# Edge counting in a graph layer: one-hots built by 16-bit comparisons of several steps, digits scaled by ScalarE, and a new order of the steps

## The reference

```
h = x @ W                                   # 1250 x 768
e = leaky_relu(e_src[src] + e_dst[dst])     # one value for each of 41250 edges (+ one self loop per node)
w = exp(e - max over the edges of one dst)
out[dst] = sum over its edges of h[src] * w / z[dst]
x = x + gat(relu(gat(layernorm(x), ...)))
```

## Time and profile before

| | |
|---|---|
| three runs | 1528.14, 1528.83, 1533.79 us |
| profiled execution | 1530.04 us, of which the span from first to last instruction is 1528.3 us |
| busy over the span | PE 92%, PE weight loads 87%, VectorE 76%, ScalarE 63%, GpSimd 32% |
| granted TensorE clock, mean | 0.972 |

### The profile page before, as it was taken

The page is one execution under the profiler, slowest core; times in us unless marked ns, Lnnn a source line. Parts: engine busy times, 40 slices in busy tenths (PEclk is TensorE's granted clock), DMA queues, the critical chain, the costliest instruction groups (busy, mean ns, idle before and its releaser), DMA issues.

```text
span 1528.3 us, 25668 instructions
## 1 busy us (share of the span) xinstructions
PE 1411.6 (92%) x8981; PEld 1336.4 (87%) x8981; DVE 1153.9 (76%) x1756; ACT 969.3 (63%) x1658; POOL 492.4 (32%) x366
## 2 busy tenths in 40 slices
PE   3998799999799999999999999999999998699996
PEld 1897577999699999899898998999988898599996
DVE  5788979735689762486877878778788787788885
ACT  7997787523368432366848767478587522599995
POOL 1000000000000010244625536256356501288886
PEclk9999799999899999999999999999999998799999
DMA  7001000122214540000000000000001496466652
GB/s 201 2 1 37 5 14 18 52 99 73 101 55 131 182 142 22 1 21 1 1 21 0 21 0 0 21 0 0 21 1 32 119 295 169 126 155 163 164 94 35
DMA packets 52312, 99.09 MB, mean 65 GB/s; under 512 B 10848, under 2 KB 26852, under 8 KB 52224
## 3 DMA queue, kind: packets, MB, share of 16 engines
q1 hardware_dynamic: 39769, 72.55, 15.4%
q0 software_dynamic: 11376, 22.29, 7.4%
q10 hardware_dynamic: 1079, 3.13, 0.7%
HBM read 67.15 MB, written 44.31 MB: 73 GB/s over the span
## 4 chain that ended last, share of the span: by engine, by line
PE 68%; DVE 9%; issue 3%; DMA 1%; ACT 1%; POOL 1%; POOLq 0%; SPq 0%; ACTq 0%; DVEq 0%
PE ps L372 14%; PE ps L373 14%; PE ps L374 14%; PE ps L823 4%; PE ps L864 4%; PE ps L843 3%; PE ps L866 3%; PE ps L845 3%; PE ps L865 3%; DVE mcol L1072 2%; PE ps L1257 1%; PE ps L598 1%; DVE prlo L1035 1%; PE ps L832 1%; PE ps L1669 1%
## 5 line engine op out<-in xcount | busy, mean ns | idle before, releaser
L1035 POOL TENSOR_TENSOR prlo<-prob,prhi 125x500 fp32r<-125x500 f32 x180 | 251.7, 1404 | 267.4 <-ACT prob L976 266.2
L1072 DVE TENSOR_REDUCE mcol<-ps 125x1 f32<-125x1250 f32 x120 | 174.9, 1458 | 72.6 <-PE ps L823 72.0
L974 ACT ACTIVATE prhi<-ps 125x500 fp32r<-125x500 f32 x300 | 176.9, 590 | 71.0 <-PE ps L845 64.9
L864 PE MATMUL ps<-prhi,vhi 125*128 125x250 f32 x600 | 172.2, 287 | 8.5 <-POOL prlo L1035 4.3
L976 ACT ACTIVATE prob<-ps 125x500 f32<-125x500 f32 x300 | 176.5, 588 | 0.6 <-DVE prlo L1035 0.6
L1524 POOL MEMSET q<- 128x2500 f32 x1 | 2.2, 2187 | 529.4 <-PE ps L374 529.4
L866 PE MATMUL ps<-prlo,vhi 125*128 125x250 f32 x600 | 168.6, 281 | 0.0
L865 PE MATMUL ps<-prhi,vlo 125*64 125x250 f32 x600 | 167.6, 279 | 0.0
L843 PE MATMUL ps<-qst,kst 128*125 128x250 f32 x600 | 155.9, 283 | 3.5 <-issue 1.4
L372 PE MATMUL ps<-hhi,pthi 125*125 125x384 f32 x400 | 153.6, 384 | 3.0 <-DVE ptlo L712 3.0
L1669 PE MATMUL ps<-ohs,ohd 128*125 128x417 bf16 x380 | 126.1, 384 | 32.4 <-DVE ohs L2112 29.6
(11 more groups left out here) (330 smaller groups left out, 4023.1 us busy)
## 6 DMA issues: line engine op xcount, KB each, us to landing
w1all<-in_L_ffn_W_dram SPq DMA_DIRECT2D x8, 1152.0 KB, 10.1
w2st<-in_L_ffn_W_dram SPq DMA_DIRECT2D x8, 1152.0 KB, 6.6
wqst<-in_L_ffn_Wqkv_dram SPq DMA_DIRECT2D x12, 384.0 KB, 4.2
hid_d<-tin SPq DMA_DIRECT2D x10, 375.0 KB
hin<-hid_d SPq DMA_DIRECT2D x10, 375.0 KB
vtin<-xn_d SPq DMA_DIRECT2D x10, 375.0 KB
out_dram<-accr POOLq DMA_DIRECT2D x10, 375.0 KB, 8.8
xres<-in_x_dram SPq DMA_DIRECT2D x10, 336.0 KB
```

Of the source, the lines that this page charges most:

```text
L864: pe.matmul(ps[:, b:b + GQ], vhi[:, e, kt, :], hi, start=kt == 0, stop=False)
L974: act.activation(prhi[:, n % RING, :], bank(3 + n % 3, P, 2 * GQ), ACT.Exp, scale=float(HD) ** -0.5)
L1035: eng.tensor_tensor(prlo[:, n % RING, :], prob[:, n % 3, :], prhi[:, n % RING, :].bitcast(f32), ALU.subtract)\
L1072: dve.tensor_reduce(mcol[:, e, t:t + 1], ps[0:P, 0:N], AX.X, ALU.max, negate=True).then_inc(sem("max"), 1)
```

## The change

The one-hots of both sides are now plain comparisons of two 16-bit tensors on VectorE, several steps in one instruction. `iota2` holds each column number twice, `drel` and `scol` are f16 in place of f32, and the two steps of a pair lie interleaved, element by element. `destinations(b)` writes 14, 12 or 12 steps at once (30 instructions of 1750 or 1500 elements, ring of 4); the sources are written 4 steps at once (10 instructions per tile, the last with 2 steps; ring of 3). The digit `sval` no longer goes into `ohs`: ScalarE multiplies it into `ohd`, in place, one instruction for each step (`valued`, in place of `apart`), and PE waits for `valued` at each step. PE reads both one-hots with a step of two elements. Edges are the first DMAs, x tile 0 and W follow on the same queue, and the chain that makes `scol` and `sval` is ahead of the test of the edges. Row tiles now take 8 steps each from g = 8 (was 13 from 31), the first turn begins at g = 111 (was 208) and a turn takes 36 steps (was 32), with other slots for its parts.

```diff
-WIDE = 420
-BATCH = WINDOW // 2
-OHS = 12
+DST_AT, DST_WIDE, DSTS = (0, 14, 26, WINDOW), 14, 4
+SRC_WIDE, SRCS = 4, 3
-FIRST, PERIOD = 31, 13
-TURN0, TURN, EARLY, SLOTS = 208, 32, 12, 21
-AHEAD = 30
+FIRST, PERIOD, PARTS = 8, 8, 13
+TURN0, TURN, EARLY, SLOTS = FIRST + 103, 36, 12, 21
+AHEAD = 20
+COUNT_READY = 8
 def linear(t, r):
-    return FIRST + PERIOD * t + r
+    return FIRST + PERIOD * (PARTS * t + r) // PARTS
+WEIGHT1_AT = (2, 3, 5, 6, 9, 10)
...
-    ohs = put("ohs", [128, OHS, WIDE], bf16, at=WEND)
-    scol = put("scol", [128, NCOLS], f32, at=put.end)
-    drel = put("drel", [128, T, WINDOW], f32, at=put.end)
+    ohs = put("ohs", [128, SRCS, SRC_WIDE // 2, PACK, 2], bf16, at=WEND)
+    ohd = put("ohd", [128, DSTS, DST_WIDE // 2, P, 2], bf16, at=ohs_end)
+    iota2 = put("iota2", [128, PACK, 2], f16, at=put.end)
+    scol = put("scol", [128, NCOLS], f16, at=put.end)
+    drel = put("drel", [128, T, WINDOW], f16, at=put.end)
...
 PE, step_near:
-                pe.wait_ge(sem("oh_ready"), g + 1)
-                pe.matmul(into, hots(b)[:, i, :], ohs[:, g % OHS, 0:PACK], start=u == 0, stop=u == WINDOW - 1).then_inc(sem("oh_free"), 1)
+                if i == 0:
+                    pe.wait_ge(sem("oh_ready"), b + 1)
+                pe.wait_ge(sem("valued"), g + 1)
+                pe.matmul(into, hot_dst(g), hot_src(g), start=u == 0, stop=u == WINDOW - 1).then_inc(sem("oh_free"), 1)
...
 ScalarE:
-                last = act.activation(hots(b)[:, i, :], iota[:, 0:P], ACT.Identity, bias=drel[:, j, u:u + 1])
+                act.activation(hot_dst(g), hot_dst(g), ACT.Copy, scale=sval[:, q:q + 1]).then_inc(sem("valued"), 1)
...
 VectorE, destinations and step_near:
-                dve.tensor_scalar(hots(b), hots(b), 0.0, None, ALU.is_equal).then_inc(sem("ohd_ready"), 1)
+                dve.tensor_tensor(ohd[:, b % DSTS, 0:pairs, :, :],
+                                  iota2[:, 0:P, :].rearrange("p (o c) z -> p o c z", o=1).broadcast_to([128, pairs, P, 2]),
+                                  drel[:, j, DST_AT[i]:DST_AT[i + 1]].rearrange("p (b o z) -> p b o z", o=1, z=2)
+                                  .broadcast_to([128, pairs, P, 2]), ALU.is_equal).then_inc(sem("ohd_ready"), 1)
-                if g >= OHS:
-                    dve.wait_ge(sem("oh_free"), g + 1 - OHS)
-                dve.tensor_scalar(ohs[:, g % OHS, :], iota[:, 0:WIDE], scol[:, q:q + 1], sval[:, q:q + 1], ALU.is_equal, ALU.mult)\
+                if b >= SRCS:
+                    dve.wait_ge(sem("oh_free"), src_end(b - SRCS))
+                dve.tensor_tensor(ohs[:, b % SRCS, 0:wide // 2, :, :], iota2[...], scol[:, q:q + wide] ..., ALU.is_equal)
...
 VectorE, first_layer:
-                        if g == (linear(t - 2, 1) if t >= 2 else 6 + 14 * t):
+                        if t and g == linear(t - 2, 1):
                             rstd1(t)
-                        if g == turn_at(t - 2, 2):
-                            leaky(dve, 0, t)
-                        if g == turn_at(t - 3, 5):
+                        if g == turn_at(t - 2, 16):
                             far_max(dve, order, 0, t)
+                        if g == turn_at(t - 2, 20):
+                            leaky(dve, 0, t)
-                        if g == turn_at(t - 2, 17):
+                        if g == turn_at(t - 1, 4):
                             weigh(dve, 0, t)
 PE: turned(t) from turn_at(t - 1, 0) to turn_at(t - 1, 6);  ScalarE: sloped(t) from turn_at(t - 2, 1) to turn_at(t - 2, 16)
```

More of the change, by code:

```diff
@@ L79, in count_bank, with dst_batch, dst_start, src_batch @@
     return 2 if j % 2 == 0 and counted_at(j) + 12 < turn_at(-1, 0) else 3
+def dst_batch(g):
+    j, u = divmod(g, WINDOW)
+    i = sum(u >= at for at in DST_AT[1:-1])
+    return 3 * j + i, u - DST_AT[i]
+def dst_start(b):
+    return WINDOW * (b // 3) + DST_AT[b % 3]
+def src_batch(g):
+    j, u = divmod(g, WINDOW)
+    return SRC_BATCHES * j + u // SRC_WIDE, u % SRC_WIDE
+def src_end(b):
+    return WINDOW * (b // SRC_BATCHES) + min(SRC_WIDE * (b % SRC_BATCHES + 1), WINDOW)
 class Order:
@@ L206, in build @@
     lohi = put("lohi", [128, 3, ECOLS], f32, at=put.end)
+    digit = put("digit", [128, 3, NCOLS], f32, at=put.end)
     xres = put("xres", [P, 2, D], f32, at=W2AT)
@@ L337, in two, with hot_dst, hot_src @@
             return ps[0:rows, b * BANK:(b + 2) * BANK].rearrange("p (a c) -> p a c", a=2)[:, :, 0:cols]
-        def hots(b):
-            return ohd2[:, :, :] if b % 3 == 2 else ohd[:, b % 3, :, :]
+        def hot_dst(g):
+            b, i = dst_batch(g)
+            return ohd[:, b % DSTS, i // 2, :, i % 2]
+        def hot_src(g):
+            b, i = src_batch(g)
+            return ohs[:, b % SRCS, i // 2, :, i % 2]
         def rows(j):
@@ L1352, in _ @@
             weights2(1)
-            for t in range(5):
+            for t in range(7):
                 row_out(t)
[L1355 to L1358, removed]
+            for k in range(2, KD):
+                weights2(k)
+            row_out(7)
             row_in(0)
             row_in(1)
-            row_out(7)
             row_out(8)
@@ L1699, in first_layer @@
                     for j in range(T):
-                        if not near and g == counted_at(j) + 18:
+                        if not near and g == counted_at(j) + COUNT_READY:
                             tile_all(j)
                     for t in range(T):
-                        if g == (linear(t - 1, 0) if t else FIRST - 7):
+                        if t and g == linear(t - 1, 0):
                             transposes1(t)
-                        if 0 <= g - linear(t, 0) < 2 * KD:
-                            triple1(t, g - linear(t, 0))
+                        for i in range(2 * KD):
+                            if g == linear(t, i):
+                                triple1(t, i)
                     if g == NINE + 2:
@@ L1809, in _ @@
             stats(0)
-            stats(1)
-            act.wait_ge(sem("set_pool"), TABLES)
-            for g in range(BATCH):
-                apart(g)
-            for g in range(BATCH, AHEAD):
-                apart(g)
+            act.wait_ge(sem("start_dve"), VALUES)
+            for g in range(4):
+                valued(g)
+            normed(0)
+            for g in range(4, 8):
+                valued(g)
+            higher1(0)
+            for k in range(KD):
+                weights1(k)
+                if k % 2:
+                    valued(7 + k // 2 + 1)
+            for g in range(11, 16):
+                valued(g)
+            stats(1)
+            for g in range(16, AHEAD):
+                valued(g)
             for g in range(SCHEDULE):
@@ L2151, in first_layer @@
                         dve.sem_inc(sem("oh_free"), WINDOW)
-                    if g in range(4, 4 * KD + 4, 4):
-                        weight1(g // 4 - 1)
+                    for b in range(2, 3 * T):
+                        if g == max(dst_start(b) - 26, 0):
+                            if near:
+                                destinations(b)
+                            else:
+                                dve.sem_inc(sem("ohd_ready"), 1)
+                    if g in WEIGHT1_AT:
+                        weight1(WEIGHT1_AT.index(g))
                     for t in range(T):
-                        if g == (linear(t - 2, 1) if t >= 2 else 6 + 14 * t):
+                        if t and g == linear(t - 2, 1):
                             rstd1(t)
-                        if g == (linear(t - 1, 12) if t else FIRST - 2):
+                        if g == (linear(t - 1, 12) if t else 1):
                             lower1(t)
```

167 lines of the change are left out of this document (86 added, 81 removed).

## The result

The changed kernel takes **1563.07 us** (median of 4 runs, 1561.38 to 1565.96) beside 1528.84 us before, a ratio of 1.0223 with a 95% interval of 1.0209 to 1.0237: slower by 34 us, where I had forecast 1513. The profiled execution took 1561.38 us with a span of 1559.1. All ratios in this document leave out slow executions, and so does the median of the run with `stats(1)` early, of whose six executions one took 2792.54 us (with it the median is 1535.16).

A forecast was written before the change was run, and what follows sets the result against it. Bounds: VectorE and ScalarE nearly always busy at the start, PE in row tiles, VectorE in turns with steps. Start -6.1, row tiles -8.0, hole -15.4, turns +13.9 give -15.6 us: 1514.4, or 1513 against the median; range 1506 to 1520, wider 1500 to 1529.

The forecast's parts named there:

- the price of the one-hots: VectorE's one-hot work per tile of 38 steps: 12.15 us with the new comparisons, 12.8 us before.
- I take 0.545: VectorE's new 16-bit comparison: 0.545 ns per element, taken from `ohs`, between ends of 0.26 and 1.03.
- The comparison runs at the f32 rate: Rival, 10 in 100: VectorE's one-hots at 1.03 ns per element, 22.1 us a tile, 1595 us in all, slower.
- my 19.0: Turns with 36 steps: 19.0 us each, VectorE the bound at 18.65, PE 18.0, ScalarE 17.6.
- 7.44 equal turns: Turns after the hole: 268/36 = 7.44 at 19.0 us, then 2.56 at 11.63; 170.6 us, 13.9 more than before.
- Turns keep their losses: Rival, 17 in 100: turns still lose 2.3 us over VectorE's work, 20.95 us each; 14.5 us of gain gone, 1527.5.
- The idle 11 us in `rstd1(1)`: Start: VectorE idle from 18.8 to 29.8 us, as `rstd1(1)` waits for `stats(1)` on ScalarE.
- the first triple: End of the start: first triple can start at 37.8 us instead of 43.9, 6.1 us less.
- The row tiles: Ten row tiles after the start: PE bound at 8.4 us each, 87.7 us in all, 8.0 less than before.
- ScalarE's parts up to the end of `stats(1)`: Start, from 19.4 us: `higher1(0)`, six parts of W, eight `valued`, then `stats(1)`, ending at 29.8 us.
- the hole: From the last row tile's end to turn 0: 22.9 us instead of 38.3, 15.4 less; first turn at 148.4 us.
- the wait for the sources of step 112: End of the hole: step 112 waits for the 834-element batch behind `far_max(1)`, a batch and `leaky(1)`, 4.9 us.

The follow-up runs named there:

- the run with turns of 38 and 18 steps: Against the kernel before: changed kernel plus even first columns, `stats(1)` directly behind `stats(0)`, turns of 38 steps, `COUNT_READY` 18 instead of 8; 1526.26 us (0.9983).
- the next run: Changed kernel with first columns rounded down to even and `stats(1)` on ScalarE directly behind `stats(0)`; 1534.00 us, 1.0038 of the kernel before.

## Why the prediction was wrong

**The step that failed** is the one in the price of the one-hots: "I take 0.545". For tiles 0 to 2 and 7 to 9 it was right (0.52). For tiles 3 to 6 the rate was 1.04, which is the rate of my rival *The comparison runs at the f32 rate*, in four tiles of ten. I had treated the rate as one property of the instruction, with one chance. It is a property of each operand's address too, and the addresses stood in the code: `STARTS` has four odd entries, and a pair of `scol` read from there does not begin on 4 bytes. The comparisons at this rate add 36 x 0.87 = 31.3 us of VectorE, all behind 150 us, and 1.8 us more in the four short ones. Nearly all of this lies in four turns of which VectorE is busy 98.0 of 98.7 us. Putting them right gave back 23.6 us (26.3 between the traces). The trace of before holds no such instruction; what could have been done is to ask for each operand in which tiles it may fall to the other end, and to put a case between 1513 and 1595 into the range.

The page that I set against my value (the Trainium skill, Vector Engine (DVE) Microarchitecture Reference, 5.1) says also that 4-byte alignment makes no difference with two sources; the comparisons with `iota2` or `ohd` shifted agree (1.02 and 1.07 us), those with the pairs of `scol` shifted do not (1.89), and the measurement decides. The Trainium skill (VectorE: DVE Perf Modes, Mode 2×_1P) asks for 4-byte alignment; by that the odd tiles are slow, as measured, and the shifted `iota2` should have been too, which it was not.

**The turns, beyond the rate.** With even columns five turns from 158 to 253 us took 18.5 to 19.6 us each, so my 19.0 stands as a number. My reason for it, that VectorE is the bound, does not: from 177.4 to 253.5 us VectorE was busy 18.2 us a turn and PE 18.7, for which I had 18.0, and the turn from 215.43 us took 18.47 us with PE busy all of it. In the run with turns of 38 and 18 steps PE waits for `ohs` nowhere from 150 to 290 us, while VectorE waits for PE:

```profile
DVE ohs L2164 <- PE ps L1710: 8.3, 8, 1.9
```

That 19.0 came out is in part luck. What I also had wrong is that all turns are alike: I counted 7.44 equal turns and then 11.63. The one from 253.5 to 274.5 us took 21.0, the next 23.0, the next, nearly without steps, 15.7. Turns of 38 steps took 8 us off (7.6 with odd columns). This is the first rival, *Turns keep their losses*, by another mechanism, and its 14.5 us were more than the 8 that came.

**The start.** The idle 11 us in `rstd1(1)` were predicted and are there. The cast and `iota2` were not: I had no term for GpSimd's new instruction. `drel` was 3.2 us later than I had it, and the first triple 3.8. The row tiles (85.5 for 87.7 us) gave 2.2 us of that back. Two of my sums don't add up as stated: 2.5 and 2 us beyond ten tiles of 8.4 give 88.5 us for the row tiles, not 87.7, and ScalarE's parts up to the end of `stats(1)` give 29.4 us, not 29.8.

**Right as sized:** `valued`, 428 ns long and 0.29 apart (13 in 3.91 us); the PE bound row tiles; the hole, with PE's clock at 0.71 in it; the wait for the sources of step 112 ahead of turn 0. With even columns the turn 0 that follows the hole took 8.3 us for its first 10 steps, not 5.3 (19.0 x 10 / 36): its granted clock was 0.50 (1.2 GHz) from 149.8 to 157.0 us and 1.00 behind, after the hole in which PE was busy 12.9 of 22.7 us. I had no term for that. Nor had I one for PE's strided operands: the count matmul takes 350 ns at the median where it took 341, 9 ns in each of 380, or 3.4 us of PE in all.

**The sum.** 50.1 us of miss: 23.6 from the odd columns (26.3 by the traces); 7.6 to 8.4 from the turns of 36; 1.4 from the start as it reaches turn 0; about 3 from the cold beginning of turn 0. Behind the first layer the profiled run lost 1.6 us more than before, and its median lies 1.7 us above it, where before it was 1.2 below. That leaves some 6 to 10 us, in part the wait for `hin` (2.2 us), that I can't settle. What also stays open: in the run with even columns the median is 3.3 us above the profiled run. A fall of the clock in the turn from 274.5 us, as in the trace of the next run (2.6 us), may be a part of it; no trace of this kernel shows it.

## What to carry to other kernels

When a price rests on a faster rate, list for each operand the tiles in which its address or shape could take it out of that rate; a window that begins at a rounded column is even only by luck. Look at the shortest and longest of a group before its mean: 1369 ns was no duration of any instruction here. If two loops are woven together, a period that does not match the other's (36 and 38) is harmless at first and costs at the end, and a new small instruction on an idle engine has to be priced too.

## What the runs showed of the hardware

A 16-bit comparison of two tensors on VectorE, 1668 elements in and out, takes 1.02 us, and 1.89 when the source that repeats a pair begins 2 bytes past a multiple of 4; the same shift of the other source changes nothing, nor does that of the output in the comparisons of 1500 and 1750 elements. GpSimd's iota of 834 elements with each number twice took 4.65 us, while 1252 numbers each once took 1.18 to 1.33. The copy on VectorE that replaced the first took 1.00 us, with small GpSimd instructions beside it. PE's granted clock fell to 0.50 for 3 to 7 us behind a wait of 3.22 us in two traces, and not behind the same wait in a third. VectorE's cast of 768 numbers, 0.56 us alone, ended only 0.41 or 0.42 us after the iota that it met, in three kernels. The Trainium skill (SBUF — State Buffer, 🔬 SBUF: two separate sides) has the port pair that the two engines share as an exclusive lock for the whole instruction of whichever starts first, where VectorE's instruction is in a two-port mode. These traces agree, if the cast is such a one: the iota began first in all three, by 0.3 to 3.2 us.
